# Softmax inverses and layer-norm roots from a ScalarE logarithm and exponential with one Newton step on VectorE, in a fused attention and expert layer

## What is computed

```python
shift = silu(t) @ W_ada.T + b_ada
h = ln(x, ln1_g, ln1_b) + shift
qkv = (h @ Wqkv.T).reshape(b, n, 3, H, HD)
q = ln(qkv[:, :, 0], qn_g, qn_b); k = ln(qkv[:, :, 1], kn_g, kn_b); v = qkv[:, :, 2]
attn = softmax(q @ k.T / sqrt(64))
x = x + (attn @ v) @ Wout.T
gate = softmax(x @ Wgate.T)
vals, idx = top_k(gate.T, tokens / 8)        # each expert takes its best 512 tokens
y = fc2(gelu(fc1(ln(x[idx], mlp_g, mlp_b)))) * vals
x = x.at[idx].add(y)
```

## Time and profile before

| what | value |
|---|---|
| three runs, median | 1293.33 us (1288.46 to 1294.29) |
| the profiled execution | 1290.78 us |
| its span | 1288.8 us |
| granted TensorE clock, mean | 0.949 |
| busy: TensorE, VectorE, ScalarE, GpSimd | 1107.9, 1043.5, 626.6, 565.6 us |
| attention stage | from 0 to about 982 us |
| one batch in the loop | 58.2 us (the variances of unit 4 start at 435.07 and again at 493.27 us) |

### The profile page before, as it was taken

How to read it: one execution, slowest core, us unless ns; L and a number is a source line. 1 busy time by engine, 2 the same in 40 slices (tenths; PEclk the granted TensorE clock), 3 DMA queues, 4 the chain that set the end, 5 groups by cost and what they waited for, 6 DMA issues and landing times.

```text
span 1288.8 us, 24533 instructions
## 1 busy us (share of the span) xinstructions
PE 1107.9 (86%) x8291; PEld 855.0 (66%) x8291; DVE 1043.5 (81%) x1956; ACT 626.6 (49%) x1002; POOL 565.6 (44%) x507
## 2 busy tenths in 40 slices
PE   4689999999999999999999999999975046999996
PEld 3457676767767676767767676767753044888886
DVE  8688988888898988888898988888886863767773
ACT  4445555556465556555464655555441003544531
POOL 3465544444454544444453544454451202345342
PEclk9799999999999999999999999999998556999999
DMA  4000000000101000000001000000003121355322
GB/s 171 9 1 18 18 18 17 16 16 16 33 0 33 16 16 16 16 16 16 27 5 33 16 16 16 16 16 16 9 25 136 42 74 35 99 160 132 102 38 29
DMA packets 32277, 48.50 MB, mean 38 GB/s; under 512 B 7920, under 2 KB 28528, under 8 KB 30960
## 3 DMA queue, kind: packets, MB, share of 16 engines
q1 hardware_dynamic: 26096, 39.49, 9.4%
q0 software_dynamic: 6144, 8.52, 3.7%
HBM read 35.29 MB, written 12.71 MB: 37 GB/s over the span
## 4 chain that ended last, share of the span: by engine, by line
PE 62%; DVE 22%; issue 8%; POOL 4%; ACT 2%; DMA 2%; DVEq 0%; ACTq 0%; POOLq 0%
PE ch L444 10%; PE ch L446 9%; PE ch L445 9%; PE av L1270 7%; PE sc L1295 7%; DVE rec L1123 4%; PE sc L1286 4%; PE av L1274 3%; PE pq L1248 3%; DVE qn L807 3%; POOL out L541 2%; PE mx L1306 2%; DVE var L1165 2%; POOL got L529 1%; DVE hit L694 1%
## 5 line engine op out<-in xcount | busy, mean ns | idle before, releaser
L899 POOL TENSOR_TENSOR qk_lo<-qkT,qk_hi 128x512 fp32r<-128x512 f32 x128 | 165.3, 1291 | 272.8 <-ACT qk_hi L965 272.8
L1123 DVE RECIPROCAL rec<-av 128x256 f32<-128x256 f32 x128 | 224.5, 1754 | 45.6 <-PE av L1274 45.0
L977 ACT ACTIVATE prob<-sc 128x1024 f32<-128x1024 f32 x128 | 131.4, 1027 | 236.6 <-PE sc L1295 236.6
L894 POOL TENSOR_TENSOR prob_sum<-prob 128x512 f32<-128x512 f32 x128 | 165.1, 1290 | 140.6 <-ACT prob L977 140.6
L444 PE MATMUL ch<-w_hi,hT_lo 128*128 128x512 f32 x384 | 174.1, 453 | 6.6 <-DVE w_lo L1045 6.5
L1270 PE MATMUL av<-prob,V 128*64 128x256 f32 x1024 | 141.0, 396 | 43.6 <-DVE oT L1125 41.6
L1145 DVE TENSOR_REDUCE m<-mx 128x4 bf16<-128x1024 f32 x128 | 155.4, 1214 | 0.0
L445 PE MATMUL ch<-w_lo,hT_hi 128*128 128x512 f32 x384 | 153.9, 401 | 0.0
L446 PE MATMUL ch<-w_hi,hT_hi 128*128 128x512 f32 x384 | 153.0, 398 | 0.0
L1270 PEld LDWEIGHTS av<-prob,V 128*64 128x64 f32 x1024 | 65.7, 137 | 101.4 <-issue 81.3
L1081 DVE TENSOR_REDUCE ssum<-sq 128x8 f32<-128x512 f32 x128 | 84.8, 680 | 55.3 <-ACT sq L944 53.5
(11 more groups left out here) (189 smaller groups left out, 2752.0 us busy)
## 6 DMA issues: line engine op xcount, KB each, us to landing
fcw<-experts SPq DMA_DIRECT2D x8, 2048.0 KB, 9.0
x_sb<-x SPq DMA_DIRECT2D x16, 256.0 KB, 2.8
xr_sb<-x SPq DMA_DIRECT2D x16, 256.0 KB, 2.7
out<-tok SPq DMA_DIRECT2D x16, 256.0 KB, 2.2
rows_dram<-xh SPq DMA_DIRECT2D x16, 256.0 KB, 2.2
prob<-w_qkvT SPq DMA_DIRECT2D x2, 512.0 KB, 7.1
qn<-w_qkvT SPq DMA_DIRECT2D x2, 512.0 KB, 7.8
V<-w_qkvT SPq DMA_DIRECT2D x2, 512.0 KB, 7.6
```

The source lines that it names most:

```text
L894: nc.gpsimd.tensor_tensor(prob_sum[(hp - 1) % 2][:, :, :], pr[:, :, 0, :], pr[:, :, 1, :], ALU.add).then_inc(prob_summed, 1)
L899: nc.gpsimd.tensor_tensor(qk_lo[par][:, :], qkT[par][:, :], qk_hi[par][:, :].bitcast(F32), ALU.subtract).then_inc(lo_ready, 1)
L977: nc.scalar.activation(prob[hp % 2][:, :], sc[:, :], ACT.Exp, scale=HD ** -0.5).then_inc(prob_ready, 1)
L1123: chain(nc.vector.reciprocal(rec[:, :], av[:, N:2 * N]))
```

## The change

For every pair, the inverse of the row sums is no longer VectorE's reciprocal. ScalarE takes the logarithm of the sums and then the exponential of its negative (`rec`), and VectorE makes one Newton step of it: `err` = sums times `rec`, `o_raw` = product times `rec`, and (`err` - 2) times `o_raw`, which is the result with its sign turned; the sign is turned back where the output projection is subtracted from `xr_sb` instead of added. The high part `o_hi` is copied by ScalarE.

For the reciprocal roots, VectorE ends units 0 and 4 with the variances; ScalarE takes the logarithm and the exponential of minus half of it in the unit after (`power_guess`), and VectorE makes one Newton step there (`refine`), behind that unit's division. The row `xh` of the next batch, in unit 1, now stands behind the division and behind `refine`. The condition's silu uses an exponential where it used tanh.

```diff
@@ scalar, batch @@
+                    if (hp == 1 and (cur or nxt) and not (isinstance(b, int) and b < 0)) or (hp == 5 and (nxt or prv) and not (isinstance(b, int) and b == B)):
+                        power_guess(b, hp - 1)
+                    if (cur and hp > 0) or (hp == 0 and prv):
+                        need(attended, u)
+                        need(error_done, u - 1)
+                        need(divided, u - 1)
+                        nc.scalar.activation(log_sum[:, :], av[:, N:2 * N], ACT.Ln).then_inc(log_done, 1)
+                        need(log_done, u)
+                        nc.scalar.activation(rec[:, :], log_sum[:, :], ACT.Exp, scale=-1.0).then_inc(inverse_ready, 1)
                     if cur:
                         need(scored, u + 1)
                         need(attended, u - 1)
                         nc.scalar.activation(prob[hp % 2][:, :], sc[:, :], ACT.Exp, scale=HD ** -0.5).then_inc(prob_ready, 1)
+                    if (cur and hp > 0) or (hp == 0 and prv):
+                        need(normed, u)
...
+                        nc.scalar.activation(o_hi[:, (hp - 1) % UNITS, :], oT[(hp - 1) % 2][:, :], ACT.Copy).then_inc(o_hi_ready, 1)
@@ power_guess, refine @@
+                need(var_ready, count)
+                nc.scalar.activation(log_var[:, 0:n], var[:, 0:n], ACT.Ln).then_inc(log_var_done, 1)
+                need(log_var_done, count)
+                nc.scalar.activation(guess[:, 0:n], log_var[:, 0:n], ACT.Exp, scale=-0.5).then_inc(guess_ready, 1)
...
+            chain(nc.vector.scalar_tensor_tensor(a, y, -0.5, y, ALU.mult, ALU.mult))
+            chain(nc.vector.tensor_tensor(a, a, v, ALU.mult))
+            nc.vector.scalar_tensor_tensor(dst[:, 0:n], a, 1.5, y, ALU.add, ALU.mult).then_inc(rstd_ready, 1)
@@ vector, batch @@
+                    if (cur and hp > 0) or (hp == 0 and prv):
+                        need(o_split, u - 2)
+                        need(inverse_ready, u)
+                        o = oT[(hp - 1) % 2]
+                        nc.vector.tensor_tensor(err[:, :], av[:, N:2 * N], rec[:, :], ALU.mult).then_inc(error_done, 1)
+                        nc.vector.tensor_tensor(o_raw[:, :], av[:, 0:N], rec[:, :], ALU.mult).then_inc(divided, 1)
+                        need(error_done, u)
+                        need(divided, u)
+                        nc.vector.scalar_tensor_tensor(o[:, :], err[:, :], 2.0, o_raw[:, :], ALU.subtract, ALU.mult).then_inc(normed, 1)
+                    if (hp == 1 and (cur or nxt)) or (hp == 5 and (nxt or prv) and not last_entry):
...
+                        refine(chain, NH + (2 if hp == 1 else 4), rstd[1 if hp == 1 else 0])
                     if hp == 1 and nxt:
...
-                    if (cur and hp > 0) or (hp == 0 and prv):
-                        need(attended, u)
-                        need(divided, u - 1)
-                        need(o_split, u - 2)
-                        chain(nc.vector.reciprocal(rec[:, :], av[:, N:2 * N]))
-                        o = oT[(hp - 1) % 2]
-                        nc.vector.tensor_tensor(o[:, :], av[:, 0:N], rec[:, :], ALU.mult).then_inc(divided, 1)
-                        need(divided, u)
...
-                        nc.vector.tensor_copy(o_hi[:, (hp - 1) % UNITS, :], o[:, :]).then_inc(normed, 1)
```

More of the change, by code:

```diff
@@ L977, in batch @@
                         nc.scalar.activation(prob[hp % 2][:, :], sc[:, :], ACT.Exp, scale=HD ** -0.5).then_inc(prob_ready, 1)
+                    if (cur and hp > 0) or (hp == 0 and prv):
+                        need(normed, u)
+                        if hp == 1 and prv:
+                            need(slot_filled, through("slot", b, (0, 2)))
+                        nc.scalar.activation(o_hi[:, (hp - 1) % UNITS, :], oT[(hp - 1) % 2][:, :], ACT.Copy).then_inc(o_hi_ready, 1)
                     if live:
@@ L991, in _, with refine @@
             over_batches(act, batch)
[L992 to L1007, removed]
+            phase23_scalar(act, power_guess)
+        def refine(chain, n, dst):
+            v, y, a = var[:, 0:n], guess[:, 0:n], na[:, 0:n]
+            chain(nc.vector.scalar_tensor_tensor(a, y, -0.5, y, ALU.mult, ALU.mult))
+            chain(nc.vector.tensor_tensor(a, a, v, ALU.mult))
+            nc.vector.scalar_tensor_tensor(dst[:, 0:n], a, 1.5, y, ALU.add, ALU.mult).then_inc(rstd_ready, 1)
         @block.vector
@@ L1016, in silu_of_condition @@
             def silu_of_condition():
[L1018 to L1020 removed]
+                dve.wait_ge(cond_exp_done, 1)
+                chain(nc.vector.tensor_scalar(sig[:, :, :], sig[:, :, :], 1.0, None, ALU.add))
+                chain(nc.vector.reciprocal(sig[:, :, :], sig[:, :, :]))
+                nc.vector.tensor_tensor(silu[:, :, :], sig[:, :, :], condT_sb[:, :, :], ALU.mult).then_inc(silu_ready, 1)
                 dve.wait_ge(con_in, 16)
@@ L1071, in last_rows @@
                 row_stats(tok, 2)
-                chain(nc.vector.tensor_scalar(var[:, NH + 2:NH + 4], mv[:, 2:4, 1], EPS, None, ALU.add))
-                rsqrt(chain, NH + 4, rstd[0])
-                token_rows(B)
+                nc.vector.tensor_scalar(var[:, NH + 2:NH + 4], mv[:, 2:4, 1], EPS, None, ALU.add).then_inc(var_ready, 1)
+                need(guess_ready, through("newton", B - 1, 4) + 1)
+                refine(chain, NH + 4, rstd[0])
+                need(rstd_ready, through("newton", B - 1, 4) + 1)
+                for t in range(TT):
+                    ins = nc.vector.tensor_scalar(xh2[:, t, :], tok[:, t, :], mv[:, 2 + t, 0:1],
+                                                  rstd[0][:, NH + 2 + t:NH + 3 + t], ALU.subtract, ALU.mult)
+                ins.then_inc(xh2_ready, 1)
             def head_sums(b, hp, pos):
@@ L1166, in batch @@
                         at = 0 if hp == 0 else 2
-                        chain(nc.vector.tensor_scalar(var[:, NH + at:NH + at + 2], mv[:, at:at + 2, 1], EPS, None, ALU.add))
-                        if hp == 0 and cur:
-                            need(qn_pool_ready, b * 2)
-                        if hp == 4 and (cur or nxt):
-                            need(qn_pool_ready, b * 2 + 1)
-                        rsqrt(chain, NH + at + 2, rstd[1 if hp == 0 else 0])
-            per = 37
+                        nc.vector.tensor_scalar(var[:, NH + at:NH + at + 2], mv[:, at:at + 2, 1], EPS, None, ALU.add).then_inc(var_ready, 1)
+            per = 11
             def counted(b, cur, nxt, prv):
```

40 lines of the change are left out of this document (29 added, 11 removed).

## The result

The changed kernel takes 1329.74 us (median; 1328.64 to 1330.31), the kernel before 1293.24 us (1288.46 to 1294.29): a ratio of 1.028, 95% interval 1.027 to 1.030. It is slower by 2.8%; the forecast was 1299.7 us in a range that ended at 1318. The kernel before, timed again beside each group of later runs, took 1290.9 to 1291.6 us, so differences of some 2 us between kernels of different groups say nothing.

What follows compares the result with a forecast made beforehand. Bound: TensorE carries 62% of the chain, so only its waits count. Looped batches +14, last batch -5.6, start -2 give +6.4 us; on the 1293.3 us median that is 1299.7 us, range 1281 to 1318.

Steps and rivals of the forecast that it cites:

- Units 5 and 6: TensorE's 2.2 us wait moves from the product to the sums, behind `prob_sum`; net 0.1 us earlier a batch.
- Unit 1: New TensorE wait for `xh`, late behind division and `refine`: 1.57 us a batch, bounds 0.67 and 2.8.
- Unit 3's: TensorE's wait of 0.52 us for the maxima goes, as reciprocal and cast ahead of them are gone.
- At nothing: ScalarE's extra work a unit, 0.84 us for the inverse and 0.42 for the copy, lies in its waits.
- per batch: Net of the looped batch's terms: +0.95 us, +14 us in 15 batches.
- Last batch: From unit 2 on VectorE sets the pace without chunks: 5.6 us saved, bounds 2 and 8.
- Start: Fewer small root instructions, twice ahead of batch 0 with TensorE idle: 2 us saved, bounds 0 and 2.8.
- `prob_sum` did not get in ahead of `qn`: Rival in unit 6: next `prob_sum` precedes `qn`'s last part, 18 us more, 1318 us; chance 0.20.
- The wait of unit 1: Rival: TensorE's new wait there is hidden, 15 x 1.05 falls out, 1284 us; chance 0.14.
- The clock: Rival: TensorE drops to its lower clock level after unit 1's new pause, 18 us more, 1318 us; chance 0.06.
- The faster rival: In unit 6 `prob_sum` escapes `rstd`'s delay if roots precede the division: 28 us less, 1272 us; chance 0.08.

Runs made afterwards that it cites:

- ohi_last: Changed kernel with ScalarE's `o_hi` copy moved behind the unit's second chunk, same work: 1300.9 us.
- division: Changed kernel's division with the reciprocal roots of the kernel before: 1262.1 us.
- roots: Changed kernel's reciprocal roots with the division of the kernel before: 1342.1 us.
- first1: Changed kernel with `refine` and `xh` ahead of the division in unit 1, the roots' guess at the end of unit 0: 1310.9 us.
- first5: Changed kernel with `refine` ahead of the division in unit 5 only: 1290.9 us.
- both: Changed kernel, `refine` (and `xh`) ahead of division in units 1 and 5, guess at end of unit 0, `o_hi` copy behind second chunk: 1237.3 us.
- poolwait: Changed kernel with GpSimd's `qn` of unit 1 waiting until VectorE's `xh` pair has ended: 1339.9 us.

## Why the prediction was wrong

- **Units 5 and 6** were right. The product's wait went, the sums wait 2.01 us for `prob_sum`, `rstd` comes 3.86 us after the start of the 128x2 variances (forecast 4.05), and the rotation waits 0.45 us for `qn` (forecast: asked for at 446.2, ready at 446.7). From unit 5's scores to unit 7's a batch gains 0.3 us (forecast 0.1).
- **Unit 1** was right in place and chain: `xh` begins 3.50 us after the start of the sums, as worked out (468.55 to 472.05). The term was mis-sized in the duration of the `xh` pair: 1.63 us from batch 0, measured 2.50. The prediction read the 0.90 us on top of 0.73 as the price of `qn` alone. In batch 0 a cast of 0.46 us stood behind `qn`, in the loop a `prob_sum` of 1.31 us, and the pair is held to its end. TensorE is 2.32 us later than before (forecast 1.57): +0.75 a batch.
- **Unit 3's** wait went, for a gain of 0.36 us (forecast 0.52).
- **"At nothing"** is the step that failed. I summed ScalarE's extra work and found room for it, but did not ask what `o_hi`'s wait holds up behind it on ScalarE. It holds up the second chunk, its head sum and the maxima: +1.33 us a batch in unit 4. ohi_last took this wait away without taking any work away. The wait needs the collision too: where unit 3's `oT` was not stretched (division), it did not appear.
- With these two the step "per batch" reads 0.95 + 0.75 + 1.33 = 3.03 us; measured 3.04. That it fits this closely is luck in part: unit 3 gained 0.16 less than forecast and units 6 and 7 about 0.2 more, and these cancel. Fifteen times 3.04 is 45.6, not 14.
- **Last batch**: the six units take 28.09 us (forecast 27.3), and 1.2 us are lost just ahead of the sums of unit 2 (forecast 0.7): 4.5 us saved instead of 5.6. That the six units alone are 5.65 us shorter only looks like the forecast. **Start**: -1.0 up to the first transposes, -1.0 in the period behind it (49.9 to 48.9); forecast -2.
- **Rivals.** `prob_sum` did not get in ahead of `qn`. The wait of unit 1 was not hidden. The clock cost 1 us in two of the looped periods (0.97 instead of 1.00) and 2.5 us in one (0.92; it took 63.73 us), not 18 in all; it became large only in roots and first1. The faster rival's condition, the roots ahead of the division, is the order of first5: it gave 39 us against the changed kernel (its price was 28 against the forecast).

## What to carry to other kernels

When work moves to an in-order engine that has room, ask first what stands behind each new wait in its queue, and put the copies that feed the bottleneck ahead of it: here the order alone, with the same instructions, is worth 92 us between the changed kernel and both. "Room" is not enough: ScalarE was busy for 58% of the span, and still one wait in its queue cost 29 us. Take the duration of an instruction that collides from the loop, with all that the other engine has queued at that moment, not from a lone pair elsewhere. And test the parts of a change apart: as first placed, the division's half won 2.3% here and the roots' half lost 4.1%; with the order changed, the roots' half too won 2%, and both together won 4.2%.

## What the runs showed of the hardware

- One VectorE pair can be held by two GpSimd instructions in a row: 2.50 us for 0.73, each of its two instructions by one of GpSimd's. The Trainium skill, "SBUF — State Buffer", section "Who interferes with whom", has the exclusion for a whole instruction, and the rows here agree; that a pair goes from one GpSimd instruction into the next is seen in unit 1.
- It hits tiny instructions as hard: the 128x32 variances take 0.17 us or, beside a `qk_lo` of 1.27, 1.25 us. With `prob_sum` 0.10 us ahead `oT` takes 1.47 us, with both at the same 0.01 us 0.42. The start alone does not tell who is held: in unit 1 the `xh` pair begins 0.03 us ahead of `qn` and is held all the same. Taken away in one place, the exclusion comes back in another (poolwait).
- The granted clock fell to 0.51 behind a wait of 2.0 us in first1 and stayed there for some 6.6 us, while the same wait left it at 1.00 in an undisturbed batch of the changed kernel.
